# Which half step computes which rest of the exponentials in layer 0

## The reference

```python
text, ip = encoder_hidden_states[:, :77], encoder_hidden_states[:, 77:]
q, k, v = heads(x @ Wq.T), heads(text @ Wk.T), heads(text @ Wv.T)
k_ip, v_ip = heads(ip @ Wk_ip.T), heads(ip @ Wv_ip.T)
out = softmax(q k^T / sqrt(16)) v + softmax(q k_ip^T / sqrt(16)) v_ip
x = out @ Wo.T + bo + x
```

## Time and profile before

| | us |
|---|---|
| median of 3 runs (lowest, highest) | 1653.78 (1650.42, 1655.32) |
| time of the profiled execution | 1653.78 |
| its span, first to last instruction | 1651.9 |

### The profile page before, as it was taken

How to read it: one execution, slowest core, us unless ns; L and a number is a source line. 1 busy time by engine, 2 the same in 40 slices (tenths; PEclk the granted TensorE clock), 3 DMA queues, 4 the chain that set the end, 5 groups by cost and what they waited for, 6 DMA issues and landing times.

```text
span 1651.9 us, 25857 instructions
## 1 busy us (share of the span) xinstructions
PE 1556.8 (94%) x7936; PEld 1182.3 (72%) x7936; DVE 1274.3 (77%) x3548; ACT 1093.0 (66%) x2319; POOL 558.9 (34%) x1313
## 2 busy tenths in 40 slices
PE   6899999999999899999999989999999999999993
PEld 3565489999556459999756538999965654899981
DVE  3698378987789549999769936888887983799975
ACT  1597378885389448888439926888826973788860
POOL 0343044443044224444115403444403430444430
PEclk9899999999999999999999999999999999999995
DMA  9110310010411230000221131000030113000100
GB/s 319 40 43 18 105 62 21 20 36 1 125 35 44 65 104 20 20 26 26 76 59 40 46 105 53 25 20 21 22 125 20 45 32 105 20 20 20 36 1 16
DMA packets 67536, 84.15 MB, mean 51 GB/s; under 512 B 29236, under 2 KB 38212, under 8 KB 67400
## 3 DMA queue, kind: packets, MB, share of 16 engines
q1 hardware_dynamic: 64728, 77.38, 15.9%
q10 hardware_dynamic: 2672, 5.13, 0.9%
HBM read 41.75 MB, written 34.10 MB: 46 GB/s over the span
## 4 chain that ended last, share of the span: by engine, by line
PE 75%; DVE 10%; ACT 9%; issue 3%; SPq 2%; DMA 2%; POOL 0%; POOLq 0%; ACTq 0%; DVEq 0%
PE ps_w L1024 42%; PE ps_s L1024 14%; PE ps_t L1024 11%; PE ps_b L1024 5%; DVE probsT_low L776 3%; ACT probs L592 3%; ACT probsT_high L573 2%; ACT probsT L581 2%; DVE row_max L839 2%; PE ps_b L1158 2%; DVE probs L863 1%; DVE stat L848 1%; ACT probs L607 1%; PE ps_m L1024 1%; DMA slots<-out_all 1%
## 5 line engine op out<-in xcount | busy, mean ns | idle before, releaser
L573 ACT ACTIVATE probsT_high<-ps_t 128x512 fp32r<-128x512 f32 x640 | 385.0, 602 | 90.5 <-PE ps_t L1024 90.4
L776 DVE TENSOR_TENSOR probsT_low<-probsT,probsT_high 128x512 fp32r<-128x512 f32 x560 | 379.3, 687 | 17.5 <-ACT probsT L581 12.4
L581 ACT ACTIVATE probsT<-ps_t 128x512 f32<-128x512 f32 x640 | 387.9, 606 | 0.0
L1024 PE MATMUL ps_w<-gram,probsT_high 128*128 128x416 f32 (+2 forms) x1280 | 383.1, 310 | 0.0
L1024 PE MATMUL ps_w<-gram_low,probsT_high 128*128 128x384 f32 (+2 forms) x1280 | 352.0, 304 | 0.0
L500 POOL TENSOR_SCALAR exp_bias<-row_max 128x1 f32<-128x1 f32 x320 | 137.1, 429 | 536.2 <-DVE row_max L839 536.2
L607 ACT ACTIVATE probs<-ps_s,exp_bias 128x508 f32<-128x508 f32 x320 | 220.8, 691 | 130.0 <-POOL exp_bias L500 89.1
L1024 PE MATMUL ps_s<-slots 96*128 96x512 f32 x640 | 280.7, 481 | 22.8 <-DVE row_max L791 9.3
L1024 PE MATMUL ps_t<-slots 98*128 98x512 f32 x640 | 251.8, 413 | 1.2 <-DMA slots<-row_max 0.2
L1024 PEld LDWEIGHTS ps_w<-gram_low,probsT_high 128*128 128x128 f32 (+1 forms) x1280 | 242.0, 189 | 6.5
L1024 PE MATMUL ps_w<-gram,probsT_low 128*128 128x400 f32 (+2 forms) x1280 | 246.1, 314 | 0.0
(11 more groups left out here) (170 smaller groups left out, 2014.1 us busy)
## 6 DMA issues: line engine op xcount, KB each, us to landing
slots<-parts SPq DMA_DIRECT2D x128, 192.0 KB, 3.3
parts<-probsT_high SPq DMA_DIRECT2D x16, 512.0 KB, 4.2
parts<-probsT_high SPq DMA_DIRECT2D x24, 256.0 KB, 4.0
parts<-probsT_low SPq DMA_DIRECT2D x8, 512.0 KB, 3.6
parts<-x_sb SPq DMA_DIRECT2D x8, 512.0 KB, 3.9
slots<-probsT_high SPq DMA_DIRECT2D x24, 128.0 KB, 3.3
parts<-probsT_low SPq DMA_DIRECT2D x12, 256.0 KB, 3.7
ctx_sb<-in_ctxT ACTq DMA_DIRECT2D x3, 1024.0 KB, 5.5
```

The source lines that it names most:

```text
L573: nc.scalar.activation(probsT_high[1 - par][:, t, :], ps_t[:, t % 2, :], ACT.Exp, scale=SCALE)
L581: nc.scalar.activation(probsT[:, t, :], ps_t[:, t % 2, :], ACT.Exp, scale=SCALE).then_inc(pt_block[l], 1)
L776: nc.vector.tensor_tensor(probsT_low[1 - par][:, t, :], probsT[:, t, :], probsT_high[1 - par][:, t, :].bitcast(F32), ALU.subtract).then_in ...
L1024: return nc.tensor.matmul(out, lhsT, rhs, start=start, stop=stop)
```

## The change

POOL takes the rest of block 3 in place of that of block 1, and does so at the end of its step, behind the value slot. DVE takes the rest of block 1, between the maxima of (n+3, first half) and L822; it no longer takes the rest of block 3 between the two groups of maxima. PE's third low matmul moves ahead of the pair for (n+3, first half), and its fourth waits for POOL's semaphore. The waits of ACT and PE are renumbered to match: the semaphore `low_second` becomes `low_last`.

```diff
--- before.py
+++ after.py
@@ -227,7 +227,7 @@
         st_block = [sem(f"st_block{l}") for l in range(2)]
         pt_block = [sem(f"pt_block{l}") for l in range(2)]
         low_block = [sem(f"low_block{l}") for l in range(2)]
-        low_second = sem("low_second")
+        low_last = sem("low_last")
         maxT_done = sem("maxT_done")
         shift_in = sem("shift_in")
         rows_in = [sem(f"rows_in{i}") for i in range(SLOTS)]
@@ -441,7 +441,7 @@
             nc.gpsimd.memset(ident[:, :], 0.0).then_inc(filled, 1)
             nc.gpsimd.memset(ones[:, :], 1.0).then_inc(filled, 1)
             nc.gpsimd.memset(out_all[:, 0:1], 0.0).then_inc(out_moved, CREDIT)
-            nc.gpsimd.memset(out_all[:, 1:2], 0.0).then_inc(low_second, CREDIT)
+            nc.gpsimd.memset(out_all[:, 1:2], 0.0).then_inc(low_last, CREDIT)
             for i in range(2 * SLOTS):
                 nc.gpsimd.memset(out_all[:, 2 + i:3 + i], 0.0).then_inc(slots_in[i // SLOTS][i % SLOTS], CREDIT)
             pool.wait_ge(filled, 2)
@@ -450,11 +450,6 @@
 
             def step0(b, n, k, turn, use, transposed, scores, scores_next, last=FIRST):
                 par = k % 2
-                if transposed:
-
-                    pool.wait_ge(pt_block[0], TB * (HEADS * b + n + 1) + 2 + CREDIT1)
-                    nc.gpsimd.tensor_tensor(probsT_low[1 - par][:, 1, :], probsT[:, 1, :],
-                                            probsT_high[1 - par][:, 1, :].bitcast(F32), ALU.subtract).then_inc(low_second, 1)
                 if scores:
 
                     pool.wait_ge(oT_moved, HEADS * b + n + 1 + CREDIT) if use else None
@@ -471,6 +466,11 @@
                         last = nc.gpsimd.tensor_tensor(v0_slot[par][:, blocks, low], src, v0_slot[par][:, blocks, cols].bitcast(F32),
                                                        ALU.subtract)
                     last.then_inc(v0_in, 1)
+                if transposed:
+
+                    pool.wait_ge(pt_block[0], TB * (HEADS * b + n + 1) + TB + CREDIT1)
+                    nc.gpsimd.tensor_tensor(probsT_low[1 - par][:, TB - 1, :], probsT[:, TB - 1, :],
+                                            probsT_high[1 - par][:, TB - 1, :].bitcast(F32), ALU.subtract).then_inc(low_last, 1)
 
             def values_of(b, head, par):
 
@@ -574,10 +574,10 @@
 
                 if l == 1:
                     act.wait_ge(low_block[1], TB * g + t + 1 + CREDIT)
-                elif t != 1:
-                    act.wait_ge(low_block[0], (TB - 1) * g + max(t, 1) + CREDIT)
+                elif t < TB - 1:
+                    act.wait_ge(low_block[0], (TB - 1) * g + t + 1 + CREDIT)
                 else:
-                    act.wait_ge(low_second, g + 1 + CREDIT)
+                    act.wait_ge(low_last, g + 1 + CREDIT)
                 nc.scalar.activation(probsT[:, t, :], ps_t[:, t % 2, :], ACT.Exp, scale=SCALE).then_inc(pt_block[l], 1)
 
             def step0(b, n, k, turn, use, transposed, scores, scores_next, last=FIRST):
@@ -800,8 +800,6 @@
                     maxima0(b, 0, 0, 0)
                 if scores:
                     maxima0(b, n + 2, 1, par)
-                if use:
-                    lowT(b, 0, n - 1, 1 - par, 3)
                 if first:
                     maxima0(b, 1, 0, 1)
                 if outputs:
@@ -815,6 +813,9 @@
                     maxima0(b, n + 3, 0, 1 - par)
                 if outputs:
                     output(last, 1)
+                if transposed:
+                    lowT(b, 0, n, par, 1)
+                if outputs:
                     output(last, 2)
                 if use:
 
@@ -1097,10 +1098,10 @@
                     mm(ps_w[par][0:V0S, :], v0_slot[par][:, t, :], probsT_high[par][:, t, :], t == 0, False)
 
                 def values_low(t):
-                    if t != 1:
-                        pe.wait_ge(low_block[0], (TB - 1) * g + max(t, 1) + CREDIT)
+                    if t < TB - 1:
+                        pe.wait_ge(low_block[0], (TB - 1) * g + t + 1 + CREDIT)
                     else:
-                        pe.wait_ge(low_second, g + 1 + CREDIT)
+                        pe.wait_ge(low_last, g + 1 + CREDIT)
                     return mm(ps_w[par][0:V0S, :], v0_slot[par][:, t, :], probsT_low[par][:, t, :], False, t == TB - 1)
 
                 first, second = not use and not transposed, not use and transposed
@@ -1136,10 +1137,10 @@
                 if use:
                     values_low(0)
                     values_low(1)
+                    values_low(2)
                 if scores_next and not first:
                     scores_half(3, 0)
                 if use:
-                    values_low(2)
                     values_low(3).then_inc(oT_done, 1)
                 if transposed:
                     scoresT_of(0, g, k, 2)
```

## The result

The changed kernel takes 1665.99 us (median of 6 runs, 1662.46 to 1670.63) against 1653.86 for the kernel before on the same chips (6 runs): a ratio of 1.0068, 95% interval 1.0050 to 1.0088, so 12.1 us slower. Its profiled execution took 1668.66 us with a span of 1666.7, 14.8 longer than that of before. Both kernels have executions with a mean granted clock of 0.985 to 0.986 and others with 0.980 to 0.983, which are some us longer. All those of the changed kernel on record with 0.986 (12, beyond the 6 above too) take 1662.5 to 1664.1 us; those of the kernel before with 0.985 or 0.986 (5, from the runs beside the experiments) take 1649.4 to 1652.0. So at equal clock the loss is about 12 us as well.

A forecast was written before the change was run, and what follows sets the result against it. The prediction took a chain from engine to engine in layer 0 to bound the kernel; 12.8 us from full periods, 1 from batch starts and 1.2 from batch ends made 15.0, so 1653.8 became 1668.8 us, range 1657 to 1678.

The forecast's parts named there:

- What bounded the kernel: Layer 0: a chain through DVE, PE's pair, low matmuls, ACT's copy and transposes sets the 4.95 us step.
- The subtraction taken from between the maxima gives back only 0.04 us: Between first and second L790: 0.60 us of work goes, but the round trip leaves 2.36 us where it was 2.40.
- The one added ahead of L822 costs its full 0.60, against 0.28 of wait saved: Second maxima to L822: the added subtraction costs 0.60 us, L822's 0.28 us wait goes; period 5.15 us.
- PE's new order is hidden: PE in full steps: the copy moves from 2.75 to 2.52 us, and PE's loop fits with 0.08 to spare.
- POOL's block 3 is in nobody's way: POOL's subtraction ends near 1.2 us of the step, ahead of DVE's block 0 subtraction at 1.48.
- The sum, 15.0 us: Whole kernel: 12.8 us from full periods, about 1 from batch starts, 1.2 from batch ends.
- the forecast of the last one: Last step of each batch: POOL's late subtraction makes the copy 0.3 us late, 1.2 us over four batches.
- The start of a batch: Step 0 of each batch: PE's pair waits 0.23 us behind the third low matmul, about 1 us in all.
- a sign of being wrong: DVE and POOL: a POOL subtraction overlapping DVE's block 0 subtraction and stretching it would refute the prediction.
- faster: Rival for full steps: the copy and transposes chain alone sets the pace, 0.23 us less a step, 1641 us; chance 0.06.
- No change: Rival for full steps: the wait moves from L822 to L790 at equal size, round trip 0.88, 1656 us; chance 0.09.
- POOL in the way: Rival for full steps: POOL's subtraction delays DVE's block 0 subtraction, 0.2 us a step, 1682 us; chance 0.06.

The follow-up runs named there:

- e7: Kernel before with only PE's order changed: low matmuls earlier, two of the next head's high matmuls ahead of the transposes; 1639.93 us, ratio 0.9919.
- e1: Kernel before with only DVE's block 0 subtraction moved behind the second group of maxima, ahead of L822; 1669.72 us, ratio 1.0080.
- e3: Changed kernel plus an unused 128x128 DVE memset between block 0's subtraction and the second L790; 1669.32 us, period 5.12.
- e4: Changed kernel plus the same unused 128x128 DVE memset between block 1's subtraction and L823; 1668.75 us, period 5.20.
- e2: Changed kernel with PE's third low matmul put back behind the pair; 1669.39 us, ratio 1.0078, period 5.12.
- e5: Changed kernel with block 2's subtraction moved between the next step's maxima and PE's third low matmul back behind the pair; 1671.44 us, ratio 1.0116.
- e8: Changed kernel with the same new PE order as e7; 1664.75 us, ratio 1.0070, period 5.11.

## Why the prediction was right, point by point

- **What bounded the kernel.** Right: the chain over pair, low matmuls, copy and transposes. Borne out by e7, which takes one low matmul (0.23 us) out of it, beside other moves on PE, and whose period is 0.23 us shorter (4.73 against 4.96, the median of before).
- **The subtraction taken from between the maxima gives back only 0.04 us.** Right: 2.36 measured, 2.36 forecast; 0.12 from the end of the pair to L790, 0.11 forecast. e1 shows that this alone makes the loss, e3 that DVE has free time there.
- **The one added ahead of L822 costs its full 0.60, against 0.28 of wait saved.** Right: 107.81 to 108.41 in the trace, and e4 shows that this gap has no idle time. The period came to 5.12, not 5.15: L823 to rest 2 is 0.35 us where it was 0.38 (L823 now starts while rest 1 is still running, to 108.49), and the rest is rounding.
- **PE's new order is hidden.** Right (e2). **POOL's block 3 is in nobody's way.** Right for the full steps: over 0.23 us ahead of rest 0. It ends 1.30 us into the step, where 1.20 was forecast and, if it had to wait for rest 2, 1.35; it meets rest 2 for 0.07 us only, so this doesn't decide between the two. Not right for the end of a batch, as shown below. e5 shows what it costs when the two meet in every step.
- **The sum, 15.0 us.** 12.1 measured between medians, 14.8 between the spans. By the profiles, the 64 full periods gave 10.1 us, not 12.8 (5.12 instead of 5.15, and the average period of before is 4.97, as some of its steps are longer than 4.95). The last three steps of a batch gave 1.2 together, the forecast of the last one, and that match is luck: in the first batch they take 4.51, 4.44 and 4.43 us against 4.74, 4.35 and 3.99, so the first of them gives 0.23 back, which the forecast didn't have.
- **The start of a batch.** Mis-sized, and for a wrong reason: not 0.23 us but 0.37 to 0.64, 1.8 in all (in the second batch 9.42 us from the L790 at 459.59, in the filling step, to the first L823, against 9.01 from 454.99 to 464.00). The forecast put it down to PE's third low matmul, but e2 takes that back and saves 0.04 at most. In the second batch it is the subtraction added ahead of L823, which is paid there too: 1.81 us from the last L790 to L823 (467.20 to 469.01) against 1.42 (462.58 to 464.00). In the first batch, with 0.64, only 0.18 comes from there (1.80 against 1.62); where the rest comes from stays open.
- **What is left over.** Together that makes 13.1 us, 1.9 less than forecast. The other 1.7 of the span lie outside layer 0; 0.83 of them are there before it begins to differ (the filling steps' L790 of 55.11 is at 55.94), so they aren't the change's. That the spans differ by 14.8, so near to the 15.0, is luck too.

The last step and the start of the second batch in the changed kernel:

```profile
159.17 0.60 ACT L581 ACTIVATE probsT<-ps_t 128x512 f32<-128x512 f32 x1
161.68 0.59 ACT L592 ACTIVATE probs<-ps_w 68x512 f32<-68x512 f32 x1 [1.90 <-PE ps_w L1025]
```

```profile
159.85 1.29 POOL L472 TENSOR_TENSOR probsT_low<-probsT,probsT_high 128x512 fp32r<-128x512 f32 x1 [3.15 <-ACT probsT L581]
```

```profile
459.59 0.32 DVE L790 TENSOR_REDUCE row_max<-ps_s 128x2 fp32r<-128x154 f32 x1 [1.93 <-PE ps_s L1025]
...
469.01 0.43 DVE L823 TENSOR_REDUCE out_all<-ps_b 128x136 f32<-128x272 f32 x1
```

From the end of ACT's last exponential (159.77) POOL takes until 161.14, and the copy starts at 161.68, where 1.91 us have passed; in the kernel before it was 1.47 (155.88 to 157.35): this handoff is 0.44 us longer, a little over the 0.3 forecast.

One step earlier POOL's subtraction does meet DVE's:

```profile
156.34 1.66 DVE L776 TENSOR_TENSOR probsT_low<-probsT,probsT_high 128x512 fp32r<-128x512 f32 x2 [1.19 <-ACT probsT L581]
```

```profile
155.41 1.29 POOL L472 TENSOR_TENSOR probsT_low<-probsT,probsT_high 128x512 fp32r<-128x512 f32 x1 [0.81 <-ACT probsT L581]
```

POOL's is over at 156.70. The first of DVE's two (rests 0 and 1, which here follow each other with no maxima between them) takes 0.92 us instead of 0.68, and so it does in this step of all four batches. The prediction had named such an overlap as a sign of being wrong; it occurs in one step of twenty, and that step is 0.09 us longer than before.

The rivals: *faster* fell with e1 and e8. *No change* needed a round trip of 0.88 us, and it takes 1.08. *POOL in the way* did not happen in the full steps of the changed kernel, but its mechanism is real: it stretches one subtraction a batch there, and it is what makes e5 the slowest.

## What to carry to other kernels

Where two engines hand a buffer back and forth, the work that stands between the release and the next use is cover for the round trip (1.08 us here). Before moving an instruction out of such a gap, compare what stays in it with the trip; before moving one into another gap, ask whether that gap had idle time of its own. Total work per engine says nothing on either: DVE has the same instructions in both kernels here.

## What the runs showed of the hardware that was not expected

A subtraction with two SBUF operands on DVE and one on POOL get in each other's way. DVE's stretched from 0.68 to 0.83 us when it met the last 0.27 us of POOL's (e1), to 0.92 when it met the last 0.36 (the changed kernel at 156.34), and two of them from 1.28 to 1.86 when the first met its last 0.70 (e5); a meeting of 0.12 (e1 at 109.04, POOL's over at 109.16) cost nothing. Each time the stretch is the overlap less 0.12 us or so, as if DVE's stood still until POOL's was over. In the other order POOL's gets longer: 1.36 us instead of 1.29 where it began at 461.89 in the changed kernel, beside a DVE subtraction of 461.45 to 462.13. DVE's reductions out of PSUM, however, ran beside POOL's subtraction at their usual length (L791 takes 1.05 us in e1's step beside POOL's 113.15, as it does in the earlier trace rows). This is in line with the Trainium skill, "SBUF — State Buffer", section "Who interferes with whom": the one that comes first holds the shared port for its whole instruction. In the kernel before, POOL's subtraction stands beside the reductions; e5 puts a price on losing that place, 0.58 us of DVE's time a step.

The answer to a wait depends on how many semaphores the instruction waits for. L790 of the first half (head n+3) waits for `s_half` and `rows_in`, and starts 0.11 us behind PE's pair, at 454.99 as it does in nearly every full step of the changed kernel. L790 of the second half (head n+2) waits for `s_half` alone and follows 0.03 to 0.04 us behind the pair, as here in the kernel before, where the pair is over at 459.91:

```profile
459.05 0.86 PE L1024 MATMUL ps_s<-slots 96*128 96x512 f32 x2 [0.84 <-DVE x_sb L782]
```

```profile
459.94 0.32 DVE L790 TENSOR_REDUCE row_max<-ps_s 128x2 fp32r<-128x154 f32 x1 [0.35 <-PE ps_s L1024]
```

That is the same instruction with the same shape, so 0.07 us of the bare round trip go with the second wait. The prediction had weighed both values, and taking the value of the earlier trace rows was the right choice. What the period would be without that wait was not tried.
